# Expert outputs of a mixture-of-experts layer added up in three DRAM sums instead of four

## The reference

```python
# B=4 batches, S=256 tokens, H=256; E=64 experts, I=96, top K=8, capacity C=128
x = x + ga * attention(layernorm(x) * (1 + ca) + sa)
h = layernorm(x) * (1 + cb) + sb
topw, topi = top_k(softmax(h @ router.T), 8)         # topw normalised to sum 1
xe[e, pos] = h[token]                                # 128 slots an expert, extra tokens dropped
g, u = split(xe @ gate_up[e])
ye = (silu(g) * u) @ down[e]
y[token] = sum over its 8 picks of topw * ye[e, pos]
out = x + gb * y
```

## Time and profile before

| | us |
|---|---|
| median of 3 runs | 340.05 (338.67 to 343.2) |
| the profiled execution | 339.45 |
| its span on the core | 337.6 |

### The profile page before, as it was taken

How to read it: one execution, slowest core, us unless ns; L and a number is a source line. 1 busy time by engine, 2 the same in 40 slices (tenths; PEclk the granted TensorE clock), 3 DMA queues, 4 the chain that set the end, 5 groups by cost and what they waited for, 6 DMA issues and landing times.

```text
span 337.6 us, 6863 instructions
## 1 busy us (share of the span) xinstructions
PE 270.1 (80%) x1855; PEld 187.5 (56%) x1855; DVE 203.1 (60%) x595; ACT 145.3 (43%) x425; POOL 172.6 (51%) x167
## 2 busy tenths in 40 slices
PE   6999999999999997997565799888987997993000
PEld 3575667556755674663222498667766776771000
DVE  3397766987699679706620176655564656653096
ACT  3456386138613861371110166455554555551000
POOL 1800000006453646467777038788878888888300
PEclk9699999999999999899559599999999999997555
DMA  7780799999999712122259699999999988866993
GB/s 233 231 274 1 201 344 334 364 382 263 312 301 286 204 70 84 58 81 95 97 170 287 168 298 300 216 199 243 233 194 218 189 142 142 126 71 70 249 294 125
DMA packets 67206, 68.78 MB, mean 204 GB/s; under 512 B 5501, under 2 KB 63698, under 8 KB 67184
## 3 DMA queue, kind: packets, MB, share of 16 engines
q1 hardware_dynamic: 55280, 52.09, 53.6%
q0 software_dynamic: 11904, 16.42, 24.9%
HBM read 37.77 MB, written 31.21 MB: 204 GB/s over the span
## 4 chain that ended last, share of the span: by engine, by line
PE 36%; DMA 28%; DVE 16%; issue 9%; ACT 6%; POOL 3%; SPq 1%; DVEq 1%; POOLq 0%; ACTq 0%
DMA sum<-stage 23%; PE bank L785 5%; PE bank L859 3%; PE bank L857 3%; PE bank L738 3%; PE bank L816 2%; DVE stage L1346 2%; PE bank L843 2%; POOL slot_rows L523 2%; DVE arena L1362 2%; PE bank L889 2%; PE bank L797 2%; DMA arena<-sum 2%; PE bank L813 2%; PE bank L854 2%
## 5 line engine op out<-in xcount | busy, mean ns | idle before, releaser
L541 POOL DMA_INDIRECT sum<-stage x60 | 92.6, 1543 | 19.9 <-issue 12.8
L523 POOL DMA_INDIRECT slot_rows<-stage x48 | 47.8, 997 | 29.5 <-issue 7.2
L1346 DVE TENSOR_SCALAR stage<-bank,stage 128x256 f32<-128x256 f32 x64 | 34.8, 543 | 38.0 <-DMA sum<-stage 33.8
L1017 PE MATMUL bank<-arena,stage 128*128 (+1 forms) x256 | 54.7, 337 | 0.0
L1017 PEld LDWEIGHTS bank<-arena,stage 128*128 128x128 f32 x256 | 41.8, 196 | 0.9 <-ACT stage L704 0.4
L1031 PE MATMUL bank<-arena,stage 96*128 (+1 forms) x128 | 41.7, 407 | 0.7 <-DVE stage L1346 0.7
L704 ACT ACTIVATE stage<-bank 128x256 f32<-128x256 f32 x64 | 24.6, 384 | 39.9 <-PE bank L1008 39.2
L738 PE MATMUL bank<-onesb 128*128 128x512 bf16 x110 | 33.9, 456 | 8.1 <-DMA slot_rows<-rows,slot_idx 5.5
L511 POOL COPY stage<-slot_idx 128x16 uint32<-128x16 uint32 x3 | 0.9, 295 | 65.1 <-DMA sum<-zero_row 57.1
L1148 DVE TENSOR_REDUCE rmax<-bank 128x2 f32<-128x512 f32 (+1 forms) x48 | 30.2, 684 | 3.2 <-PE bank L816 2.8
L589 ACT ACTIVATE arena<-bank 128x512 f32<-128x512 f32 x48 | 26.8, 598 | 5.2 <-PE bank L859 4.4
(11 more groups left out here) (152 smaller groups left out, 475.7 us busy)
## 6 DMA issues: line engine op xcount, KB each, us to landing
slot_rows<-zero_row SPq DMA_DIRECT2D x8, 1040.0 KB, 12.7
stage<-slot_rows SPq DMA_DIRECT2D x64, 130.0 KB
arena<-in_gate_up SPq DMA_DIRECT2D x10, 768.0 KB, 12.9
sum<-zero_row SPq DMA_DIRECT2D x4, 1152.0 KB, 12.1
arena<-in_gate_up SPq DMA_DIRECT2D x24, 192.0 KB
arena<-sum SPq DMA_DIRECT2D x16, 256.0 KB, 6.0
arena<-in_down SPq DMA_DIRECT2D x5, 768.0 KB, 13.4
arena<-in_down SPq DMA_DIRECT2D x12, 192.0 KB
```

The source lines that it names most:

```text
L523: pool.indirect_dma_start(slot_rows, bass.IndirectOffsetOnAxis(ap=idx[:, t, k:k + 1], axis=0), src[:, t, :], None, bounds_check=SLOTS - 1, ...
L541: pool.indirect_dma_start(sums[a], where, ye[:, j % NACC, :], None, bounds_check=ACCROWS - 1, oob_is_err=True, compute_op=ALU.add).then_in ...
L1017: last = mm(bank[2 + q % 2][:, 0:GU + 1], xeT[:, q % 2, k * CAP:(k + 1) * CAP], expert_w[:, s - 1, k * (GU + 1):(k + 1) * (GU + 1)], start ...
L1346: V.tensor_scalar(ye[:, q % NACC, :], bank[6 + q % 2][:, 0:H], gatew[:, q:q + 1], meta[:, q, 1:2], ALU.mult, ALU.mult).then_inc(v_ye, 1)
```

## The change

Three sums replace four: `NACC = 3`. The ring of output buffers keeps its four entries under a name of its own, `NYE = 4`. Expert e now adds to sum e % 3, so POOL's wait before the add (L540) is for expert e-3. DVE's waits still mean what they meant: `meta` needs the landing of e-8, `ye` that of the add four experts earlier; they now look at other semaphores (`added[e % 3]`). DVE's loop takes 24 experts a round (`TURN`, two rounds) so that e % 3 and e % 8 are both known when the code is written. SP zeroes three sums, and reads three back, in the order 0, 1, 2; DVE's closing code, unchanged in its text, adds sum 1 to sum 0 for four batches, and then goes on to sum 2, now the last. With three sums the last three adds, experts 61, 62 and 63, go to sums 1, 2 and 0. The loops of PE, ACT and SP, and the order of reads on SP, stay as they are.

```diff
--- before.py
+++ after.py
@@ -30,7 +30,8 @@
     TOK = B * S
     SLOTS = E * CAP
     ROW = H + 4
-    NACC = 4
+    NACC = 3
+    NYE = 4
     ACCROWS = TOK + CAP
     EW = HC * (GU + 1) + H
     EARLY = 32
@@ -68,7 +69,7 @@
 
 
         NXE = 8
-        stage = sb("stage", [P, NXE * (ROW + 5) + 2 * HC * CAP + 6 * I + 2 * CAP + NACC * H])
+        stage = sb("stage", [P, NXE * (ROW + 5) + 2 * HC * CAP + 6 * I + 2 * CAP + NYE * H])
 
         def region(whole, at, limit):
 
@@ -98,7 +99,7 @@
         hidT = ffn([2, CAP], parts=I)
         gatew = ffn([NXE])
         meta = ffn([NXE, 4])
-        ye = ffn([NACC, H])
+        ye = ffn([NYE, H])
 
 
         SC = TPB * S - P
@@ -538,10 +539,10 @@
                 where = bass.IndirectOffsetOnAxis(ap=meta[:, j, 2:3].bitcast(U32), axis=0)
                 if adds_before(e, a):
                     pool.wait_ge(added[a], 16 * adds_before(e, a))
-                    pool.indirect_dma_start(sums[a], where, ye[:, j % NACC, :], None, bounds_check=ACCROWS - 1,
+                    pool.indirect_dma_start(sums[a], where, ye[:, j % NYE, :], None, bounds_check=ACCROWS - 1,
                                             oob_is_err=True, compute_op=ALU.add).then_inc(added[a], 16)
                 else:
-                    pool.indirect_dma_start(sums[a], where, ye[:, j % NACC, :], None, bounds_check=ACCROWS - 1,
+                    pool.indirect_dma_start(sums[a], where, ye[:, j % NYE, :], None, bounds_check=ACCROWS - 1,
                                             oob_is_err=True).then_inc(added[a], 16)
 
             for e in range(E):
@@ -1318,13 +1319,21 @@
             slots(B - 1, (1,), B + 1, 1)
 
 
-            def expert_steps(i, j, first, last_):
-                s = GRP * i + j
+            TURN = NACC * GRP
+
+            def wait_added(turns, e):
+
+                dve.wait_ge(added[e % NACC], 16 * (GRP * turns + e // NACC + 1))
+
+            def expert_steps(turns, e, last_):
+
+                s = TURN * turns + e
+                i, j = NACC * turns + e // GRP, e % GRP
+                first = isinstance(turns, int) and e < GRP
                 if not last_:
                     dve.wait_ge(xe_ld[j], 16 * i + 16)
                     if not first:
-
-                        dve.wait_ge(added[j % NACC], 16 * (2 * i - 1 + j // NACC))
+                        wait_added(turns, e - GRP)
                     V.tensor_copy(meta[:, j, 0:3], xe[:, j, H:H + 3]).then_inc(v_meta, 1)
                 if not (first and j < 1) and not (last_ and j > 0):
                     q = (j - 1) % GRP
@@ -1340,19 +1349,18 @@
                     q = (j - 3) % GRP
                     dve.wait_ge(p_ye, s - 2)
                     dve.wait_ge(a_w, s - 2)
-                    if not (first and j < 3 + NACC):
-
-                        dve.wait_ge(added[q % NACC], 16 * (2 * i + (-1 if j < 3 else (j - 3) // NACC)))
-                    V.tensor_scalar(ye[:, q % NACC, :], bank[6 + q % 2][:, 0:H], gatew[:, q:q + 1], meta[:, q, 1:2],
+                    if not (first and j < 3 + NYE):
+                        wait_added(turns, e - 3 - NYE)
+                    V.tensor_scalar(ye[:, q % NYE, :], bank[6 + q % 2][:, 0:H], gatew[:, q:q + 1], meta[:, q, 1:2],
                                     ALU.mult, ALU.mult).then_inc(v_ye, 1)
 
             clear()
-            for j in range(GRP):
-                expert_steps(0, j, True, False)
-            with dve.Fori(1, E // GRP - 1) as i:
+            for e in range(GRP):
+                expert_steps(0, e, False)
+            with dve.Fori(0, (E - 2 * GRP) // TURN) as turns:
                 clear()
-                for j in range(GRP):
-                    expert_steps(i, j, False, False)
+                for e in range(GRP, GRP + TURN):
+                    expert_steps(turns, e, False)
             clear()
 
 
@@ -1368,10 +1376,10 @@
                 link(V.tensor_tensor(s0, s0, gbB[:, b:b + 1, :].broadcast_to([P, TPB, H]), ALU.mult))
                 return V.tensor_tensor(x_sb[:, ts, :], x_sb[:, ts, :], s0, ALU.add)
 
-            for j in range(GRP):
-                expert_steps(E // GRP - 1, j, False, False)
-            for j in range(3):
-                expert_steps(E // GRP, j, False, True)
+            for e in range(E - GRP, E):
+                expert_steps(0, e, False)
+            for e in range(E, E + 3):
+                expert_steps(0, e, True)
 
             for a in range(1, NACC - 1):
                 for b in range(B):
```

## The result

The changed kernel takes 351.37 us (median of 4 runs, 348.73 to 353.47) against 339.75 for the kernel before: ratio 1.033, 95% interval 1.027 to 1.039. I had forecast 342.4 in a range of 339 to 348, "no change". Some executions of every kernel here are slower, at a lower mean granted clock; the ratios compare the faster ones alone, the medians take all.

A forecast was written before the change was run, and what follows sets the result against it. The prediction took POOL's issue, one add every 1.85 us, to bound the expert stage, with the closing stage a second bound; +1.9 us for POOL's waits and +0.5 for the closing raised 340.05 to 342.4 us, range 339 to 348.

The forecast's parts named there:

- POOL bounds the stage: Expert stage: POOL's issue sets the pace, one add every 1.85 us, 110.4 us for 59 steps.
- part 3: POOL's wait before each add, for e-3 instead of e-4: landings over 5.47 us stall it, +1.9 us in all.
- 0.07 from landing to start: POOL's adds: time assumed from the landing waited for to the add's start, 0.07 us, read at expert 4.
- the recurrence: POOL's adds: start is the latest of previous start + 1.85, landing(e-3) + 0.07, and end of output + 0.78 us.
- the threshold: POOL's adds with three sums: landing time above which the add three experts later stalls, 5.47 us.
- Rival A: POOL's wait, experts 4 to 36: longer landings beside weight loads make it the bound, +7.2 to +9.4 us; chance 10%.
- the sign of A: Profile after the change: POOL's last add starting after 319 us would show that POOL's wait had become the bound.
- The closing: Last add's start to DVE's end: 21.5 us against 20.98, +0.5, bounds -1.9 to +3.0.
- The Trainium skill: Reads in the closing stage: its fit, 2.6 us for 256 KB, would make the closing 0.8 us shorter than forecast.
- Zero fill: Before the expert stage, 4 fills to 3: first scatter up to 2.2 us sooner, taken as worth 0.
- DVE's waits and loop: DVE in the expert stage: other semaphores and 2 rounds instead of 6, taken as 0, bounds -0.5 and +0.5 us.
- Expert 3 adds instead of writing: Start of POOL's adds: expert 3 waits for expert 0, expert 4 starts at 204.14 instead of 203.68, +0.5 us.

The follow-up runs named there:

- experiments 1: Kernel before, four sums, with POOL also waiting for expert e-3's landing before it adds e: ratio 1.017, median 345.4 against 339.5, stage 123.2 us.
- 5: Kernel before, four sums, with adds 50 to 63 also waiting for expert e-2's landing: the 13 steps took 30.1 us (one execution).
- experiment 2: Changed kernel with the sums read back and added in the order 1, 2, 0: closing 19.5 us instead of 22.6, ratio to before 1.029, median 348.6.
- experiment 3: Changed kernel with a fourth, unused array zeroed again: ratio to before 1.037, first add at 198.39 us.
- 8: Kernel before, four sums, with DVE's expert code as in the changed kernel (two rounds of 24): ratio to before 0.9995, median 348.1 us.
- experiment 4: Kernel before with the extra wait for expert e-3's landing only from expert 41 on: ratio 1.009, stage 116.4 us.

## Why the prediction was wrong

- *POOL bounds the stage, at 1.85 us an add*: right. Every kernel with four sums takes 116.1 to 116.7 us, with and without DVE's long loop, unless it waits for a nearer landing that comes late (experiments 1 and 5).
- *The wait for e-3* (part 3): the mechanism was right, its place mostly too (excess 3.8 + 3.9 us from expert 3 to 40, where the kernel before has 0.6 + 0.6; 0.5 after expert 40, where I had nothing). One term was mis-sized: "0.07 from landing to start, as at expert 4". It is 0.8 us. Expert 4 had started 0.07 us after the landing of expert *1*, which it does not wait for:

```profile
197.20 0.74 issue
...
199.36 4.25 DMA sum<-stage
...
203.68 0.80 POOL sum L541
```

 Its own releasers were expert 0's landing at 202.2 and its output, ready at 202.35 + 0.54 = 202.89; from there to 203.68 is 0.79.

```profile
202.35 0.54 DVE L1346 TENSOR_SCALAR stage<-bank,stage 128x256 f32<-128x256 f32 x1
```

 The same 0.8 stood in the recurrence for the output (0.78) and as 0.74 of "issue" in the chain before expert 0, so it comes with POOL's start, whichever of the two waits is the last. Had I used it for both, the threshold is 4.74 instead of 5.47, at the median of the earlier trace rows instead of far above it, and the same recurrence over the landings of before gives a stage of 124.2 to 124.8 us, by how the landings without a record are rebuilt. Measured: 124.0. With the rest as forecast, that is 340.05 + 8.0 + 0.5 = 348.6, still 2.8 under the median measured: 1.1 of it is the closing, the rest was not explained.
- *Rival A* was what came to pass, at the price that I gave for landings 0.6 to 0.8 us longer (+7.2 to +9.4). Its condition did not come about: landings did not grow (median of the adds with a record 4.7 before and after); their allowance shrank by 0.73, which is the same thing in the sum. I had given it 10%.
- *Bounds*: my range for the part, 0.5 to 5.2, varied the landings alone and took the 0.07 as exact, though it was read off a single case. POOL's last add starts at 325.76, after the 319 that I had named as the sign of A; 3.8 us of that are the front's.
- *The closing*: forecast 21.5, measured 22.6. The 3.8 us of last landing held (3.75). The first read took 2.8 us, not 3.4; the fifth landed at 336.92, so the first four steps took 1.15 us each, not 0.75, which I had read between the fifth and the sixteenth read. DVE's first operation so starts 11.25 us after the last add instead of 10.2, and that is the whole miss: the 11.3 us from there to its end are those of my sum, though DVE was never idle in them (16 operations), where I had it waiting up to the eighth read. That the reading order costs more than the smaller count gains is what experiment 2 shows (3.1 against 1.5).
- *The Trainium skill*, page "DMA: Bandwidth & Descriptors", section "Anatomy of one DMA — SWDGE (gpsimd) path", has a fit for DMAs that gpsimd issues, by which 256 KB take 2.6 us (an estimate). The first read behind the adds, which SP issues, took 2.8 and is near it; the fifth, issued 2.0 us later behind four others, took 5.4 and is not.
- *Zero fill and DVE's waits and loop at nothing*: right; the first by experiment 3, the last by 8. POOL's first copy now waits for DVE's slot numbers and no more for the fills.
- *Expert 3 adds instead of writing, +0.5*: the same term failed. Expert 3 started 0.83 us after expert 0's landing, so from the first add to expert 4's it took 6.95 us against 5.74 before, +1.2.

## What to carry to other kernels

In a rotation over n accumulators the test is not "landing under n pitches" but "landing plus start-up of the waiting engine under n pitches"; read that start-up from a case where the wait named is surely the one that ended last, and over several cases. A wait one step nearer costs nothing while it is met in time (experiment 4), and all that it is late beyond that, so ask which landings lie near the edge and what makes them long: here nearly all go with weight loads, which run in little more than half of the stage. When the number of accumulators changes, look at which one the last item falls to, and read that one last.

## What the runs showed of the hardware

POOL's start of an indirect DMA comes 0.8 us after the last of its waits is met, when POOL is idle: 0.82 before expert 7 of the changed kernel, 0.81 to 0.83 in 15 of its 17 adds that stood idle over 0.35 us for a landing (experts 27 and 48 took 1.6 and 1.1), and 0.78 to 0.81 after an output (experts 0 to 2). When the wait is met earlier, only 0.30 of idle time is seen behind the add before. The pitch of 1.85 us repeated in every kernel and on each of three chips. Landings of the same add range from 3.7 to 3.9 us with nothing beside them (experts 50 to 61 before) to 5 to 6.8 for the long ones beside weight loads of 192 KB.
